# Causal self-attention behind the second cross-attention: scores of four heads as two 64-row matmuls instead of one 128-row matmul

## What is computed

```python
xh = x.reshape(b, s, h, d).transpose(0, 2, 1, 3)          # h = 16 heads, d = 16, s = 64
Q, K, V = (einsum('bhsd,hde->bhse', xh, W) for W in (Wq, Wk, Wv))
scores = einsum('bhsd,bhtd->bhst', Q, K) / sqrt(d)
attn = softmax(where(causal, scores, NEG_INF), axis=-1)
out = einsum('bhst,bhtd->bhsd', attn, V)
cat = out.transpose(0, 2, 1, 3).reshape(b, s, e)
scrambled = cat.transpose(0, 2, 1).reshape(b, s, e)
x = x + scrambled @ W_O
```

## Time and profile before

| | |
|---|---|
| median of 3 runs | 3031.07 us |
| profiled execution: its time, and its span | 3030.97 us, 3029.2 us |
| PE busy, share of the span | 2598.6 us, 86% |
| DVE, ACT, POOL busy | 1550.3, 1403.8, 930.9 us |
| chain that ended last | issue 38%, PE 27%, POOL 21%, DVE 6% |
| mean granted TensorE clock | 0.928 |

### The profile page before, as it was taken

The page is one execution under the profiler, slowest core; times in us unless marked ns, Lnnn a source line. Parts: engine busy times, 40 slices in busy tenths (PEclk is TensorE's granted clock), DMA queues, the critical chain, the costliest instruction groups (busy, mean ns, idle before and its releaser), DMA issues.

```text
span 3029.2 us, 75593 instructions
## 1 busy us (share of the span) xinstructions
PE 2598.6 (86%) x32048; PEld 2161.2 (71%) x32052; DVE 1550.3 (51%) x2693; ACT 1403.8 (46%) x2563; POOL 930.9 (31%) x867
## 2 busy tenths in 40 slices
PE   6999832248999999999999999999999973699997
PEld 3555411137888888888888888888888743699997
DVE  3443377724445355455454454454454534477775
ACT  1222211125555555655655656656556431456564
POOL 1000034243443442442443443443433202211121
PEclk9999955569999999999999999999999965799999
DMA  8888500031110110100100101101101002466665
GB/s 346 316 317 314 224 0 0 0 112 42 35 35 23 35 34 23 37 32 23 45 24 25 44 23 34 35 23 35 34 23 35 2 1 96 155 215 203 213 198 154
DMA packets 48581, 270.19 MB, mean 89 GB/s; under 512 B 4896, under 2 KB 23584, under 8 KB 33696
## 3 DMA queue, kind: packets, MB, share of 16 engines
q1 hardware_dynamic: 40160, 255.82, 23.4%
q0 software_dynamic: 8160, 10.29, 2.2%
HBM read 247.58 MB, written 20.61 MB: 89 GB/s over the span
## 4 chain that ended last, share of the span: by engine, by line
issue 38%; PE 27%; POOL 21%; DVE 6%; DMA 3%; ACT 3%; POOLq 1%; SPq 0%; DVEq 0%; ACTq 0%
POOL k_lo L530 7%; POOL ctx_lo L538 6%; PE PS L1025 3%; PE PS L1005 3%; PE PS L1365 2%; PE PS L1366 2%; PE PS L1367 2%; POOL sideB L558 2%; POOL qbd_lo L543 2%; DMA unit_raw<-in_experts 1%; PE PS L1287 1%; PE PS L1382 1%; POOL slots_d L633 1%; PE PS L1384 1%; PE PS L1383 1%
## 5 line engine op out<-in xcount | busy, mean ns | idle before, releaser
L1634 DVE TENSOR_REDUCE mpart<-PS 128x1 f32<-128x802 f32 (+1 forms) x512 | 487.8, 988 | 443.2 <-PE PS L1141 443.0
L825 ACT ACTIVATE probs<-PS 128x1024 f32<-128x1024 f32 (+1 forms) x416 | 425.1, 1022 | 241.9 <-PE PS L1287 236.9
L530 POOL TENSOR_TENSOR k_lo<-sideB,k_hi 128x400 fp32r<-128x400 f32 (+1 forms) x256 | 255.2, 997 | 353.7 <-ACT k_hi L761 353.3
L538 POOL TENSOR_TENSOR ctx_lo<-ctx_raw,ctx_hi 128x801 fp32r<-128x801 f32 x128 | 224.6, 1764 | 430.2 <-ACT ctx_hi L773 430.2
L1287 PE MATMUL PS<-qbd_hi,k_hi 64*128 64x256 f32 (+1 forms) x1664 | 312.1, 372 | 0.0
L1141 PE MATMUL PS<-k_hi,qbd_hi 128*128 128x512 f32 (+2 forms) x1024 | 263.0, 359 | 22.8 <-POOL ctx_lo L538 13.7
L1153 PE MATMUL PS<-probs,vals 128*32 128x64 f32 x13312 | 272.9, 222 | 3.0 <-ACT probs L825 2.2
L760 ACT COPY sideB<-PS 128x400 f32<-128x400 f32 (+1 forms) x256 | 126.6, 494 | 275.4 <-PE PS L1121 275.4
L1153 PEld LDWEIGHTS PS<-probs,vals 128*32 128x32 f32 x13312 | 205.3, 109 | 66.5 <-ACT probs L825 14.0
L1128 PE MATMUL PS<-wkv_hi,ctx_hi 128*128 128x256 f32 (+1 forms) x832 | 236.4, 284 | 0.0
L1130 PE MATMUL PS<-wkv_hi,ctx_lo 128*128 128x256 f32 (+1 forms) x832 | 234.3, 282 | 0.0
(11 more groups left out here) (324 smaller groups left out, 6174.3 us busy)
## 6 DMA issues: line engine op xcount, KB each, us to landing
unit_raw<-in_experts SPq DMA_DIRECT2D x46, 1536.0 KB, 7.1
ctxN<-in_ctxN SPq DMA_DIRECT2D x16, 3328.0 KB, 10.8
ctxT<-in_ctxT SPq DMA_DIRECT2D x16, 3204.0 KB, 10.4
ctx_raw<-in_ctxT SPq DMA_DIRECT2D x64, 801.0 KB, 4.5
slots_d<-pad_rows SPq DMA_DIRECT2D x2, 2990.0 KB, 18.5
xg<-slots_d SPq DMA_DIRECT2D x23, 260.0 KB, 2.8
x<-in_x SPq DMA_DIRECT2D x1, 2048.0 KB, 9.6
sum_d<-x SPq DMA_DIRECT2D x1, 2048.0 KB, 6.3
```

The source lines that it names most:

```text
L530: g.tensor_tensor(k_lo[:, n, a, c:c + width], k_raw[p % 2][:, 0:width], k_hi[:, n, a, c:c + width].bitcast(F32), ALU.subtract).then_inc(s. ...
L538: g.tensor_tensor(ctx_lo[:, a, cols], ctx_raw[:, cols], ctx_hi[:, a, cols].bitcast(F32), ALU.subtract).then_inc(s.ctx_lo_ready, 1)
L825: act.activation(probs[rows, t % PROBS, :], PS[rows, 1024 * (t % 2):1024 * (t % 2) + 1024], ACT.Exp).then_inc(s.pr_ready, 1)
L1634: v.tensor_reduce(mpart[:, pair, half:half + 1], PS[:, at:at + width], AX, ALU.max).then_inc(s.mx_red, 1)
```

## The change

A quarter now holds two heads of the upper 64 rows of a half and two of the lower 64 rows. The score matmul becomes two: rows 0 to 63 of `sqT` with `skbd`, 64x256, into bank 5, and rows 64 to 127 into bank 6. `skbd` is 256 columns wide instead of 512, since upper and lower heads lie above each other in a column; its mask `tile_head` is the sum of two blocks of columns of `head_of`, made once. DVE's masking reads both banks in one instruction with one more dimension. The values take their heads by `head_in`, and `cat_of` puts the results back in place. Bank 5 also takes the values' results, so waits move: values of q = 0, 1, 2 now wait for `s4_masked` of the next quarter, and the scores of q = 2 and 3 for `weighed4_ready`.

```diff
-        skbd = [sideB[:, 1792 + 512 * n:2304 + 512 * n].rearrange("p (h t) -> p h t", h=HPQ) for n in range(2)]
+        skbd = [sideB[:, 2304 + 256 * n:2560 + 256 * n].rearrange("p (h t) -> p h t", h=2) for n in range(2)]
+        tile_head = small[:, 88:92]
+        def head_in(q, k):
+            return HPT * (q // 2) + 4 * (k // 2) + 2 * (q % 2) + k % 2
+
+        def cat_of(q):
+            half = cat[:, q // 2 * HPT * HD:(q // 2 + 1) * HPT * HD]
+            return half.rearrange("p (r q h e) -> p r q h e", r=2, q=2, e=HD)[:, :, q % 2, :, :]
+            g.tensor_tensor(tile_head, head_of[:, 0:4], head_of[:, 4:8], ALU.add).then_inc(s.tile_head_ready, 1)
...
-                g.tensor_tensor(skbd[q % 2], skT[:, a, None, :].broadcast_to([P, HPQ, P]),
-                                head_of[:, h:h + HPQ, None].broadcast_to([P, HPQ, P]), ALU.mult).then_inc(s.skbd_ready, 1)
+                g.tensor_tensor(skbd[q % 2], skT[:, q // 2, None, :].broadcast_to([P, 2, P]),
+                                tile_head[:, q % 2 * 2:q % 2 * 2 + 2, None].broadcast_to([P, 2, P]), ALU.mult).then_inc(s.skbd_ready, 1)
...
+                    elif q == 1:
+                        pe.wait_ge(s.s4_masked, T["s4_masked"].up())
                     else:
-                        pe.wait_ge(s.s4_masked, T["s4_masked"].up())
+                        pe.wait_ge(s.weighed4_ready, T["weighed4"].up())
                     pe.wait_ge(s.skbd_ready, T["skbd"].up())
-                    pe.matmul(bank(6), sqT[:, q // 2, :], skbd[q % 2].rearrange("p h t -> p (h t)"), start=True, stop=True)\
-                      .then_inc(s.s4_ps, 1)
+                    for r in range(2):
+                        part = slice(64 * r, 64 * r + 64)
+                        mm = pe.matmul(bank(5 + r, 2 * P), sqT[part, q // 2, :], skbd[q % 2][part, :, :].rearrange("p h t -> p (h t)"),
+                                       start=True, stop=True, skip_group_check=True)
+                    mm.then_inc(s.s4_ps, 1)
...
-                    if q:
+                    if q < 3:
+                        pe.wait_ge(s.s4_masked, T["s4_masked"].up())
+                    else:
                         pe.wait_ge(s.weighed4_ready, T["weighed4"].up())
-                    if q in (0, 3):
                         pe.wait_ge(s.v_ready, T["v_sb"].now())
                     pe.wait_ge(s.p4T_ready, T["p4T"].up())
                     for k in range(HPQ):
-                        mine = (q * HPQ + k) * HD
+                        mine = head_in(q, k) * HD
...
-                    v.tensor_tensor(s4[q % 2], bank(6).rearrange("p (h t) -> p h t", h=HPQ),
-                                    causal[:, None, :].broadcast_to([P, HPQ, P]), ALU.add).then_inc(s.vec_step, 1)
+                    v.tensor_tensor(s4[q % 2].rearrange("p (r h) t -> p r h t", r=2), PS[:, 512 * 5:512 * 7].rearrange("p (r h t) -> p r h t", r=2, t=P)[:, :, 0:2, :],
+                                    causal[:, None, None, :].broadcast_to([P, 2, 2, P]), ALU.add).then_inc(s.vec_step, 1)
```

More of the change, by code:

```diff
@@ L302, in build @@
             qk_ps qk_ready scores_ps nmax_ready probsA_ready pT_ps pT_ready av_ps att_ready attT_ps attT_ready outA_ps x_done
-            qkv_ps qkv_ready ss_ps snmax_ready sp_ready spT_ps spT_ready so_ps
+            tile_head_ready qkv_ps qkv_ready ss_ps snmax_ready sp_ready spT_ps spT_ready so_ps
             xq_ready xqT_ps xqT_ready diag_ready rows_ps rows_ready h_ps h_scaled conv_mid conv_done silu_done odd_scaled
@@ L553, in spread_keys @@
             def spread_keys(q):
-                a, h = divmod(q * HPQ, HPT)
                 if q >= 2:
                     g.wait_ge(s.s4_ps, s4p.up())
-                g.tensor_tensor(skbd[q % 2], skT[:, a, None, :].broadcast_to([P, HPQ, P]),
-                                head_of[:, h:h + HPQ, None].broadcast_to([P, HPQ, P]), ALU.mult).then_inc(s.skbd_ready, 1)
+                g.tensor_tensor(skbd[q % 2], skT[:, q // 2, None, :].broadcast_to([P, 2, P]),
+                                tile_head[:, q % 2 * 2:q % 2 * 2 + 2, None].broadcast_to([P, 2, P]), ALU.mult).then_inc(s.skbd_ready, 1)
+            g.wait_ge(s.tile_head_ready, 1)
             def pool_pair(first, last):
@@ L1223, in finish @@
                 if g == 16:
-                    T["s4_masked"].up()
                     pe.wait_ge(s.cat_ready, T["cat"].up())
@@ L1690, in finish @@
                     v.wait_ge(s.o4T_ps, T["o4T"].up())
-                    v.tensor_tensor(cat[:, q * HPQ * HD:(q + 1) * HPQ * HD].rearrange("p (h e) -> p h e", h=HPQ),
-                                    bank(7, P).rearrange("p (h x) -> p h x", h=HPQ)[:, :, 0:HD],
-                                    s4_inv[q % 2][:, :, None].broadcast_to([P, HPQ, HD]), ALU.mult).then_inc(s.cat_ready, 1)
+                    v.tensor_tensor(cat_of(q),
+                                    bank(7, P).rearrange("p (r h x) -> p r h x", r=2, x=32)[:, :, :, 0:HD],
+                                    s4_inv[q % 2].rearrange("p (r h) -> p r h", r=2)[:, :, :, None].broadcast_to([P, 2, 2, HD]), ALU.mult).then_inc(s.cat_ready, 1)
                 if g == 16:
```

## The result

The change takes 3006.47 us, the median of 4 runs (3006.04 to 3012.54), against 3031.99 us of the kernel before beside it: ratio 0.992, 95% interval 0.9905 to 0.9935. That is 25.5 us less; the forecast was 3001.5, 29.5 less.

A forecast was written before the change was run, and what follows sets the result against it. PE was taken to bound the kernel, with ACT near behind. Per pair 0.43 + 1.44 - 0.07 = 1.80 us, 27.0 over 15 pairs, plus 2.5 in the tail: 29.5 off 3031.0, 3001.5 us; range 2995 to 3016.

The forecast's parts named there:

- POOL's spread, PE's first wait: Ahead of the scores of q = 0, PE's 0.61 us wait for POOL's first spread shrinks by 0.43 us.
- scores, q = 0: Score matmuls of q = 0 until the next matmul take 0.55 us instead of 1.03, gaining 0.48 us.
- scores, q = 1 to 3: Score matmuls until the transposes take 0.64 us instead of 0.96, gaining 0.32 us per quarter.
- transposes, q = 1 to 3: Transposes behind the scores, 0.53 us before the change; no change in their own length was counted.
- values wait for `s4_masked`: Values on PE waiting for DVE's masking: 0.07 to 0.20 us in hand, another 0.09 gained, costed at nothing.
- ACT in step 9: PE waits for ACT's exponential in step 9, 0.05 to 0.1 us; 0.07 us per pair taken off the gain.
- The first rival: Score row halves overlap only in part (passes in program order) or not at all: 3015 or 3024 us; chance 0.13.
- I cost it at nothing: Values' wait for `s4_masked`, moved forward: another 0.09 us of room, counted as zero in the sum.
- no new wait of the values for DVE: Sign expected in the profile after: masking at 0.69 us and values on PE not newly waiting for DVE.
- the second rival: ACT becomes the bound in steps 7 to 12; a pair gains 1.2 us instead of 1.80, 3010.5 us; chance 0.07.
- The tail: Tail at the lower clock: 1.3 us saved for q = 0, 0.4 for each later quarter, 2.5 us in all.
- the moved wait: In the tail, scores of q = 2 wait for DVE's copy, 0.3 us plus two hand-overs of 0.05.

The follow-up runs named there:

- the spread made wide: The change, but POOL spreads 512 columns per quarter as before, the second half never read: 3016.05 us, ratio 0.9947 to the kernel before.
- keys first: The change, but ACT copies the keys before the queries and POOL's first spread waits for that copy only: 3005.22 us, ratio 0.9911.
- The experiment on the same rows: The change, but both score matmuls use rows 0 to 63, leaving out the lower heads' scores: 3031.3 us, ratio 0.9997.
- the scaling removed: The change without DVE's scaling instruction; queries scaled in ACT's copy, mask subtracted, minimum taken: 3004.91 us, ratio 0.9913.
- POOL's work moved: The change, but ACT rounds the last two context parts in steps 5 and 6 instead of 6 and 7: 3016.74 us, ratio 0.9949.
- the scaling moved: The change with only the scores of q = 1, 2, 3 issued ahead of the weighing: 3002.18 us, ratio 0.9899.
- the scores ahead: The change with keys copied first, no scaling, and scores of q = 1, 2, 3 ahead of the weighing: 2998.51 us, ratio 0.9884.

## Why the prediction was right, and where it was off

The direction, the main mechanism and the range held; 25.5 us came of the 29.5 that were forecast. Two terms that the working put at nothing were not nothing. Term by term, for one pair:

| term | forecast | measured |
|---|---|---|
| POOL's spread, PE's first wait | 0.43 | 0.42 in the trace, and 0.42 with the spread made wide |
| scores, q = 0 | 0.48 | 1.03 - 0.51 = 0.52 |
| scores, q = 1 to 3 | 3 x 0.32 | 3 x 0.33 |
| transposes, q = 1 to 3 | 0 | -3 x 0.055 |
| values wait for `s4_masked` | 0 | -(0.74 - 0.47) = -0.27 |
| ACT in step 9 | -0.07 | 0 |
| pair | 1.80 | 1.45 (the terms above: 1.50) |

**Scores.** The two f32 row halves run side by side, and the sizes taken from L1232, on opposite corners of the array, carried over to 64*128 within 0.01 us at q = 1 to 3. At q = 0 it was 0.51 for 0.55 behind PE's wait, and 0.54 without it (keys first). The second two of the four start 0.327 us behind the first two, where 0.33 was forecast. The first rival, passes in program order, is ruled out by the start times; its chance was 0.13. The experiment on the same rows gave what it looks like without overlap.

**Transposes.** The working had one change of shape more at q = 1 to 3 and gave it 0.10 us, all of it ahead of the transposes. The transposes themselves it left as they were, 0.53. That the first of them loses its early weight load was missing: 3 x 0.055, 2.5 us over 15 pairs.

**The step that failed: "I cost it at nothing".** The working for the wait that moved forward had two margins, 0.20 us at q = 1 and 0.07 at q = 2 (0.02 without the 0.05 that PE needs behind DVE), and treated both as DVE's own pace. The row at 950.01 had 0.32 us where the one at 945.09 had 0.17, and I did not ask why. It was the mark of POOL. When PE gets faster, the scaling starts earlier against POOL's subtraction, whose start hangs on ACT's cast; so it is stretched more, and ends at the same time, 2.93 to 2.94 us behind the start of the scores in both kernels. The forecast gave this wait another 0.09 us of room; in fact the values came 0.27 us earlier against an end that stood still. That cost 0.27 us per pair, 4 us in all, the largest part of what the forecast had too much. Of what the profile after was to show, "no new wait of the values for DVE" did not come true.

The experiments show it from three sides: the scaling removed (the gap closes, 0.21 us per pair), POOL's work moved (the stretch moves with it), the scaling moved (it grows to 1.57 us). The Trainium skill has this as a rule: SBUF — State Buffer, "SBUF: two separate sides", says that the port pair which DVE and GpSimd share is an exclusive lock, that DVE needs it in a 2-port performance mode or, against a GpSimd instruction that reads SBUF, with two SBUF inputs, and that whichever comes second is blocked for the whole of the other's instruction. The trace agrees: the ends lie 0.02 to 0.03 us apart in all three cases, and the reduction at 1170.92, which lies under the same subtraction, keeps its 0.69 us. That it is this lock, and in which mode the scaling runs, no run here shows; they show that the scaling ends with POOL.

**ACT.** The forecast named ACT in step 9 for 0.07 us; in the change it is hidden behind the values' wait. It shows once that wait is gone: with the scores ahead it holds back the transposes of step 8 by 0.15 us and those of step 6 by 0.07. As the second rival it got 0.07, and it did not happen in the change; it is next in line.

**The tail.** Forecast 2.5 us less. From the scores of q = 0 to the last matmul with `wo` it took 25.4 us before and 24.2 in the change, and the spread adds 0.43: 1.6 us less. The rows of the change for q = 0 to 2, answering to the earlier trace rows:

```profile
2460.61 1.23 PE L1209 MATMUL PS<-sideB 64*128 64x256 f32 x4 [1.80 <-POOL sideB L566]
2463.55 1.23 PE L1209 MATMUL PS<-sideB 64*128 64x256 f32 x4 [1.71 <-DVE small L1692]
2465.23 1.12 PE L1218 MATMUL PS<-ident,sideB 128*128 128x128 f32 x4 [0.45 <-ACT sideB L800]
2467.11 0.65 PE L1230 MATMUL PS<-sideB 128*32 128x128 f32 x8 [0.77 <-ACT sideB L804]
2468.17 1.23 PE L1209 MATMUL PS<-sideB 64*128 64x256 f32 x4 [0.41 <-DVE xnT L1701]
```

From q = 0 to q = 1 it is 2.94 us instead of 3.75, 0.81 less. From q = 1 to q = 2 it is 4.62; before it was 2487.18 - 2482.90 = 4.28. Here the moved wait, scores for the copy of the values, costs 0.41 us, and the transposes wait for ACT, so that faster scores gain nothing. I had this cost in the working but gave each of the three quarters 0.4 us; the one quarter lost 0.34. From q = 2 to q = 3 it is 0.46 less, and from there to the end 0.23 less.

**The sum.** From the first scores of the stage to the scores of q = 0 in the tail (15 distances, the tail's spread in the last of them) it took 1653.1 us before, 1630.5 in the first profile of the change and 1629.1 in the second: 22.6 and 23.9 less. The tail from there on gives 1.2. So 23.8 and 25.1 us are accounted for, of 25.5 measured. The steady part is 14 x 1.45 = 20.3 us. The last distance gave 1.1 in the first profile and 3.6 in the second. The last pair has no projections for a next pair, and the granted clock changes within it between its upper and its lower level: from 2420 to 2430 us it was 0.85 in the first profile and 1.00 in the second. The rest lies where nothing was changed but the one small instruction: the first scores start at 824.9 to 830.2 us in all profiles but one, and the part behind the tail takes 522.4 to 525.9. The profiles do not say why. It is enough to hide the 3 us of variants that differ by 0.2 us per pair; such variants are told apart by their pairs, not by their medians.

## What to carry to other kernels

Halving a matmul by row tiles pays only what passes side by side; put it where the neighbour has the same shape, and count each change of shape with both of its ends and with the weight load that can't go ahead any more. When a change makes one engine faster and moves a wait forward, look at how long each small instruction ahead of that wait takes at every place: one that is longer in some places than in others is itself held up, and its margin will not grow. Such an instruction can be folded into its neighbours, as the scaling was into a copy.

## What the runs showed of the hardware

- Two f32 matmuls on the upper and lower 64 rows of the array, 128 columns wide, run at the same time, both passes of each: two starts within 0.007 us, the next two 0.32 us later (at 2.4 GHz). On the same rows they stand one after the other, 1.06 us instead of 0.64 until the transposes.
- A change of tile shape cost about 0.10 us ahead of the first matmul of the new shape at 2.4 GHz; one change less, with what it costs on both sides, made a step 0.20 us shorter (2.83 to 2.63).
- Four transposes took 0.59 us instead of 0.53 whenever the weights of the first were not loaded ahead: behind a matmul of another shape, where no load went ahead, and behind one of their own shape when ACT's exponentials came late.
- DVE's scaling of 128x4 numbers between SBUF buffers took 0.17 us alone and 0.71, 0.74 and 1.57 us when it began under a subtraction of POOL, ending with it. The reduction of 0.69 us that lay under the same subtraction kept its time.
